# Attention on one Trainium2 core: the order of row score, turned maxima and column score within a TensorE step

## The reference

```
x = x + attention(group_norm(x))
x = x + sphere_conv(group_norm(x))

q = rope(split_heads(conv(Wq x + bq)));  k = rope(split_heads(conv(Wk x + bk)))
v = split_heads(conv(Wv x + bv))
a = softmax(q k^T / sqrt(256))
attention = conv_1x1(Wo (a v) + bo)
```

## The kernel before, in words

| work | first step | places modulo 32 |
|---|---|---|
| row score and its maximum | 0 | all |
| split_max | 32 | 0 |
| turn_max; keep_max; load_max | 35; 36; 37 | 3; 4; 5 |
| column score t and its exponential | 42 + t | 10 + t |
| low part of t on VectorE, t = 1, 5, 9, 23, 26, 30 | 43 + t | 12, 16, 20, 2, 5, 9 |
| mix sets, one each four steps | 54 | 22, 26, 30, 2, 6, 10, 14, 18 |
| logarithm, inverse, division | 67 and 83 | 3 and 19 |
| tail parts | 86, 88, 91, 93 | 22, 24, 27, 29 |

## Time and profile before

### The profile page before, as it was taken

One profiled execution on the slowest core, in us unless ns is written; L12 is line 12 of the kernel. 1 busy time (PEld: TensorE's weight loads), 2 busy tenths in 40 slices (PEclk: granted clock), 3 DMA queues, 4 the chain that ended last, 5 costly groups with the idle time before them and its releaser, 6 DMA issues. The chain is left out here.

```text
span 1154.9 us, 25535 instructions
## 1 busy us (share of the span) xinstructions
PE 1051.2 (91%) x10288; PEld 564.1 (49%) x10288; DVE 827.7 (72%) x1210; ACT 682.9 (59%) x1146; POOL 745.9 (65%) x768
## 2 busy tenths in 40 slices
PE   0899999999997999999999999999976888799997
PEld 0677777777773233333333333333323344354553
DVE  5888776666669988999888888888831865544343
ACT  3857677777652666666666666666664322446345
POOL 1144455545553799999999999899975129919900
PEclk9999999999997899999999999999988899999999
DMA  9934434341654939174544628191050999766661
GB/s 304 324 99 139 117 90 142 101 133 40 159 140 125 151 78 159 44 109 85 95 77 77 112 68 127 38 155 45 14 156 37 292 321 282 222 222 162 203 201 48
DMA packets 137589, 158.62 MB, mean 137 GB/s; under 512 B 17808, under 2 KB 85664, under 8 KB 137340
## 3 DMA queue, kind: packets, MB, share of 16 engines
q1 hardware_dynamic: 114368, 122.15, 44.0%
q10 hardware_dynamic: 14560, 25.66, 6.1%
q0 software_dynamic: 8544, 9.18, 3.1%
HBM read 106.11 MB, written 52.89 MB: 138 GB/s over the span
## 5 line engine op out<-in xcount | busy, mean ns | idle before, releaser
L1349 POOL TENSOR_TENSOR a_pl<-a_prob 128x512 bf16<-128x512 f32 x416 | 455.7, 1125 | 52.6 <-ACT a_prob L1306 50.8
L1306 ACT ACTIVATE a_prob<-a_col 128x512 f32<-128x512 f32 x512 | 279.7, 598 | 152.5 <-PE a_col L1217 151.9
L1265 DVE TENSOR_REDUCE a_negmax<-a_row 128x1 f32<-128x512 f32 x384 | 244.5, 679 | 40.8 <-PE a_row L1197 40.6
L548 PE MATMUL f_acc<-f_wh,f_xhl 128*32 128x384 bf16 x2560 | 163.5, 327 | 1.0 <-DVE f_yl L666 1.0
L666 DVE TENSOR_TENSOR f_yl<-f_acc,f_yh 128x768 bf16<-128x768 f32 x80 | 75.3, 956 | 75.8 <-ACT f_yh L780 75.8
L1276 DVE TENSOR_TENSOR a_pl<-a_prob 128x512 bf16<-128x512 f32 x96 | 108.4, 1130 | 24.8 <-ACT a_prob L1306 24.7
L903 POOL TENSOR_TENSOR f_straight<-f_straight,f_turned 128x832 f32<-128x832 f32 x40 | 85.5, 2137 | 59.4 <-DVE f_turned L692 59.4
L1622 PE MATMUL b_acc_s<-b_xh,b_mat_h 128*104 128x512 bf16 x256 | 99.5, 389 | 14.3 <-DVE b_xl L1706 13.2
L1197 PE MATMUL a_row<-a_k,a_q 96*128 96x512 bf16 x256 | 98.1, 383 | 10.9 <-DVE a_negmax L1265 8.9
L548 PE MATMUL f_acc<-f_wl,f_xhl 128*32 128x384 bf16 x1280 | 107.8, 326 | 0.0
L1217 PE MATMUL a_col<-a_q,a_k 98*128 98x512 bf16 x256 | 95.8, 387 | 7.6 <-DMA a_q<-a_maxrows 5.5
(11 more groups left out here) (166 smaller groups left out, 1989.6 us busy)
## 6 DMA issues: line engine op xcount, KB each, us to landing
X<-b_x ACTq DMA_DIRECT2D x16, 526.0 KB, 8.7
a_v<-V SPq DMA_DIRECT2D x16, 512.0 KB, 5.3
Z<-a_z ACTq DMA_DIRECT2D x32, 256.0 KB, 2.2
b_res<-X SPq DMA_DIRECT2D x38, 208.0 KB
out<-b_y ACTq DMA_DIRECT2D x38, 208.0 KB
V<-f_vout SPq DMA_DIRECT2D x64, 104.0 KB
b_raw<-X SPq DMA_DIRECT2D x24, 258.0 KB, 8.1
q<-in_x SPq DMA_DIRECT2D x6, 1024.0 KB, 6.5
```

What stands on the lines that cost most here:

```text
L548: last = nc.tensor.matmul(acc[half][c * KW:(c + 1) * KW, part, 0:PART], xx[g % 2][:, (half * QUAD + c) * FH + f, at], ww[half * QUAD + c][ ...
L1265: nc.vector.reduce_max(negmax[n % PAIR][:, 0, t:t + 1], row[ROW_PLACE[step][0]][:], AX.X, negate=True).then_inc(max_done, 1)
L1306: nc.scalar.activation(prob[sets_done % RING][:, t % QUAD, :], col[step % COLS][:], ACT.Exp).then_inc(exp_done, 1)
L1349: nc.gpsimd.tensor_tensor(pl[p][:, r, :], prob[p][:, r, :], ph[p][:, r, :], ALU.subtract).then_inc(lo_pool, 1)
```

## The change

Within a step TensorE now emits the row score first, then the turned maxima (at place 3 only), then the column score; before it was turned maxima, column score, row score. Mix sets and tail parts stay behind them. `row_places` hands out banks in the same new order, so at place 3 the row score takes the bank that the turn took, and the turn the next. The lists of the other engines are untouched.

```diff
@@ row_places
             for at in range(UNITS * STEPS + TAIL):
+                if EARLY <= at < UNITS * STEPS:
+                    rows[at] = take(at)
+                    maxima[rows[at][0]] = at + 1 - EARLY
                 n, t = divmod(at - TURN, STEPS)
                 if t == 0 and 0 <= n < UNITS:
                     turns[n] = take(at)
                     turned[turns[n][0]] = n + 1
-                if EARLY <= at < UNITS * STEPS:
-                    rows[at] = take(at)
-                    maxima[rows[at][0]] = at + 1 - EARLY
@@ block.tensor
-            pipeline(units(TURN, turn_max) + steps(EXP, col_scores) + rows(row_scores) + sets(MIX, mix_set) + tail_parts(TAIL, tail))
+            pipeline(rows(row_scores) + units(TURN, turn_max) + steps(EXP, col_scores) + sets(MIX, mix_set) + tail_parts(TAIL, tail))
```

## The result

The changed kernel takes 1177.49 us (median of 4 runs, 1174.27 to 1179.59) against 1159.36 for the kernel before in the same comparison (1154.14 to 1162.59): ratio 1.017, 95% interval 1.0141 to 1.0199. It is slower by 18 us; the forecast was 17 over the median it started from. The profiled execution took 1178.01 around a span of 1176.2.

What follows compares the result with a forecast made beforehand. Each unit was taken as bound by TensorE and VectorE in turn, with ScalarE's inverse releasing the divisions. Terms 7.3 + 6.2 + 3.8, plus 0.2 in the last unit, gave 17.5 us more: forecast 1174.5, range 1157 to 1183.

Steps and rivals of the forecast that it cites:

- The unit is bound by two stretches in turn: TensorE bounds places 24 to 31, VectorE place 31 to place 22; no engine fills the 31.37 us unit.
- Rival (c): Tail stretch: row scores following a mix set or tail come 0.22 sooner, so 1141 us; chance 0.10.
- Row scores lose nothing, column scores and mix sets pay: Equal work between row scores, gain 0; column scores come after the bank wait, mix sets one column score (0.22) later.
- The divisions start when ScalarE lets them: Places 3 and 19: division waits for ScalarE's inverse, starting 0.73 to 0.76 after it in all 27 divisions.
- Term 1: Place 3: column score 3 behind row score and turn makes the division 0.56 later; 13 units, 7.3 us.
- Term 2: Place 12: later exponential delays GpSimd's low part, so VectorE's waits 0.44 longer; 14 units, 6.2 us.
- Term 3: Place 19: later column score 19 makes exponential and division 0.27 later; 14 units, 3.8 us.
- Places at no cost: Bank exchange at place 3, later load of the turned maxima and later first turn: all hidden, nothing paid.
- (a): Only the divisions count, the low part at place 12 keeps its length: 11.3 us, some 1168; chance 0.21.
- (b): The change does nothing, VectorE's own queue ending the waits: unit 31.37, time 1157 us; chance 0.17.
- Rival (d): More collisions: another low part a unit goes from 1.126 to 1.558, +6 us each, two give 1186; chance 0.07.
- whatever is added ahead of the inverse lengthens the unit: Places 3 and 19: since divisions start when ScalarE lets them, delay ahead of its inverse makes the unit longer.

Runs made afterwards that it cites:

- run 8: Kernel before, with the new order at places 22 to 31 (the tail stretch) alone: 1156.83 us, ratio 0.998.
- run 9: Kernel before, with VectorE making the low part of place 5 ahead of that place's maximum: 1147.99 us, ratio 0.992.
- run 5: Kernel before, with the new order and banks at places 2 and 3 alone: 1167.19 us, ratio 1.0088.
- run 1: Changed kernel, with the old order and banks at places 2 and 3: 1166.21 us, ratio 1.009 to the kernel before.
- run 6: Changed kernel, with the inverse ahead of the exponential in ScalarE's list: 1165.46 us, ratio 1.0069 to the kernel before.
- run 2: Changed kernel, with the old order at places 18 and 19: 1175.40 us, ratio 1.0156 to the kernel before.
- run 4: Kernel before, with only the new banks at place 3 and TensorE's old order: 1157.79 us, ratio 1.0006.
- run 11: Kernel before, with ScalarE's inverse ahead of the exponential and all six VectorE low parts ahead of their places' maxima: 1147.13 us, ratio 0.9913.

## Why the prediction was right

*The unit is bound by two stretches in turn.* This holds as far as it was tried. Row score 24 to 31 kept its length (8.3), and run 8 shows that the order in the tail stretch is worth nothing either way, while run 9 gains in the other stretch by a swap on VectorE alone. Rival (c), 0.22 for each starved maximum, is out: VectorE's waits for row scores went from 3.5 to 3.6 a unit.

*Row scores lose nothing, column scores and mix sets pay.* Shown by run 5: the order at places 2 and 3 makes all of the 0.67 by itself. Run 1 alone would not show it. There 0.29 of the second distance stay, as in run 8, where the order in the tail stretch makes the split longer, from 0.34 to 0.72.

*The divisions start when ScalarE lets them.* True, but not for the reason given. The prediction took the constant 0.73 to 0.76 for the proof. The distance is as constant where VectorE's own queue ends the wait: 1.20 to 1.22 at place 3 in run 6, 0.97 to 1.00 in run 1. In a schedule that repeats, every distance repeats. What carries the claim is that the distance fell below 0.72 in no run, that VectorE stood idle in front of the division (1.22 in run 5, 0.30 in the changed kernel, 0.06 before), and that run 5 lengthened the unit by ScalarE's path alone. The margin was narrow: in the kernel before, VectorE's queue would have let the division start only 0.14 sooner at place 3 and 0.06 sooner at place 19.

*Term 1* was mis-sized: 0.56 predicted, 0.67 measured, 13 units of it 8.7 and not 7.3. What was too low is the price of the turn between two full products. Row score to turn takes 0.32, not 0.22, and turn to column score 0.35, not 0.31. Its upper bound of 0.78 held it.

*Term 2* was right in its sum, not in its place. Of the 0.44 by which row score 18 comes later, 0.12 fall on the low part of place 9 (1.25 for 1.13) and 0.32 on that of place 12. The low part of place 16 grew by 0.12 to 0.19 besides; "the delay shifts the later meetings alike" was wrong there. The Trainium skill, "SBUF — State Buffer", section "Who interferes with whom", had been weighed for this term. Its rule of an exclusive lock held in kind: the low parts grew where they met GpSimd earlier in its instruction, and run 9 took a whole meeting away. The traces of all 13 kernels say it more sharply. Of their 1248 low parts on VectorE 1114 wait for GpSimd, and each of these ends 1.58 to 1.60 us after the start of GpSimd's 1.04 us instruction, whenever it starts itself. That is also why term 2 could be worked out from a difference of starts alone: a low part that starts 0.32 nearer to GpSimd's start (0.46 behind it and not 0.78) takes 0.32 more.

*Term 3*: row score 18 to the division grew by exactly 0.27. But taking it away alone gave 0.17 (run 2), because of the low part of place 16: VectorE's third maximum from 614.55 on would free it at about 616.4, 0.1 before the division. Terms 2 and 3 come to 0.71 together against 0.70 measured. Undone one at a time they give 0.39 and 0.17, which is less than the sum, since ScalarE's path and VectorE's own queue end within some 0.1 of each other.

*Places at no cost*: the banks are shown to cost nothing (run 4). That the load of the turned maxima is hidden holds for all units but the first, where the stall comes and goes in kernels of either order.

Sum in the prediction's form: 13 x 0.67 + 14 x 0.70 = 18.5, against 17.5 predicted and 18.1 in the medians. The trace has 17.2 between the first and the last of these divisions, for two of the 27 parts do not show: the first distance "19 to 3" grew by 0.11 only, and the first unit is covered by its stall. A unit grew by 1.37 where 1.27 had been predicted, and that is the test of the account. That the medians agree to 1 us is luck in part: single executions of the kernel before lie 8 us apart, and the profiled span grew by 21.3, of which 2.9 are the first unit. The step from the sum to the forecast has a slip: 1174.3 and the 0.6 by which the profiled execution lay under the median give 1174.9 and not 1174.5. Rivals (a) and (b) are out: their units would have been 32.2 and 31.4. Rival (d) is there in small, at place 16, where VectorE still stands idle for 0.05 to 0.12 ahead of the division.

What the prediction had in the wrong form is its general sentence that whatever is added ahead of the inverse lengthens the unit. The division and the low part behind it are two joints on the same chain: ScalarE sets both, the inverse for the first and the exponential ahead of GpSimd's instruction for the second. When VectorE alone is late the second joint takes it back (runs 1 and 8, some 0.24). When ScalarE is late, it doesn't (run 5). No run made GpSimd alone late.

## What to carry to other kernels

When one engine's product feeds two others, look at what stands behind a wait on its queue: moving a product that may have to wait ahead of one that seldom does makes both wait, and where the work between two waits stays equal, as here, there was nothing to win in return. A distance between two engines that is the same in every repetition is no proof of a hand-off: it was as constant at 1.21 as at 0.75. Look at the end of the waiter's own queue as well. If it is idle in front of the wait, the releaser's path is the place to price a reorder; if the two end within 0.1 of each other, undoing one gives back only part. An instruction whose duration varies at one shape may be waiting inside: look at what another engine started shortly before. Here a swap of two neighbours on VectorE (run 9) gave 0.8% where the change had cost 1.7%.

## What the runs showed of the hardware

VectorE's low part (two SBUF inputs, 128x512) takes 0.67 to 0.69 when no instruction of GpSimd is running, or when it starts 0.9 or more behind GpSimd's. Nearer than that it ends 1.58 to 1.60 after GpSimd's start in 1114 cases, so it takes 1.52 when it starts 0.06 behind it, 1.13 at 0.46, 0.81 at 0.78. The exceptions are ten cases of run 6, where the two start within 0.02 of each other and VectorE's takes 0.67; in one more case of that run, just as near, it takes 1.56. GpSimd pays in its turn: its instruction takes 1.59 in the case of run 6 and 1.51 in run 5, where VectorE's started 0.06 ahead of it. The small split of the maxima (128x32) pays too, 0.34 to 0.77. A four-part turn of 128 columns each between two products of 512 columns takes TensorE 0.67 from the start of the row score to that of the column score, where the row score alone takes 0.22. After TensorE had stood idle for 1.32 the granted clock was 0.62 and then 0.81 over the next 6 us in the changed kernel; after 1.43 in run 11 it stayed at 1.00.
